# Row keys in the scatter's ring: from GpSimd's casts to a transfer of SyncE's

## The chip, the core and the metric

The kernel runs on one core of a Trainium2 chip. The metric is the device time of one execution in microseconds (us). The core's engines named here are TensorE (PE in the rows), VectorE (DVE), ScalarE (ACT), GpSimd (POOL) and SyncE (SP), which only issues DMA transfers. An indirect DMA is issued from GpSimd, and its descriptors are made there, so that each one is an instruction of that engine with a duration of its own; a plain DMA that SyncE issues is an instruction of SyncE's queue.

## What is computed

The model is a graph network with 6250 nodes of 256 features and 200,000 edges of 128 features. The part that the change touches is the first message sum: every edge's features are projected and added up at the edge's source node, and two tables are looked up by in-degree and out-degree.

```python
in_deg = jnp.minimum(jax.ops.segment_sum(ones, dst, num_segments=num_nodes), MAX_IN_DEGREE - 1)
out_deg = jnp.minimum(jax.ops.segment_sum(ones, src, num_segments=num_nodes), MAX_OUT_DEGREE - 1)
edge_proj = edge_attr @ W_sum + b_sum
sum3d = jax.ops.segment_sum(edge_proj, src, num_segments=num_nodes)
...
return x + z_in[in_deg] + z_out[out_deg] + cent_term + vor_term + sum3d
```

`src` is not sorted. Linear attention, a routed feed-forward layer, a second graph layer, a second attention and a mixture of experts follow; none of their code changes.

## The kernel before

**Section 1, sorting (to about 72 us).** The edge numbers lie as 128 partitions by 1568 columns (`EC`; 1562 columns are full, `EF`, and one more holds the tail of 64 edges). VectorE turns the source ids into fp32 keys (`src_f`, the first `EC` columns of the large tile `XT`) and into blocks of 125 nodes (`hi_src`), raises `hi_ready`, and counts how many edges fall into each block. It also copies the ids into the tile `pair`. SyncE loads the ids and `x`, writes a few padding rows to memory (line 357 and 358), and waits for all of that and for a barrier (line 304).

**Section 2, scatter, degree counts and attention.** The edges' rows are brought into the order of their source block by a scatter to the memory tensor `rows_by_src`. A row there has 129 words: 128 features and the source id as a key, by which a later stage builds one-hot tiles. What happens at once:

- SyncE loads features into a ring of three slots (`RINGS`), each of 11 columns (`HC`), that is 11 rows of 129 words in each partition. A slot's load waits until the eleven scatters that read it have landed (`ring_out`). There are 143 such units (`UNITS`); the last has one column.
- GpSimd's function `put_keys(n)` casts the 11 ids a partition of unit n from `pair` into word 128 of the slot's rows (line 609). It is called for unit n+1 behind the first scatter of unit n. Each unit then has 11 indirect DMAs (line 619), one a column, each of 128 rows of 516 bytes: 1563 in all.
- VectorE ranks the edges within their blocks in four chunks of columns (`CHUNKS`, lines 672 to 696), which gives the addresses `pos_src` of the scatter: a chunk must be ranked (`ranked`) before the first scatter of its columns. Then it makes one-hot tiles (`hots`) for the degree counts: 262 groups, each of two TENSOR_TENSOR instructions (lines 647 and 650), whose products TensorE sums (line 900). When all groups are done, it copies the counts (line 711), and the rest of the section (statistics, q, k and v, attention) follows from there as one chain.

The ranking and most of the one-hot work run beside the scatter. The section ends with a barrier, and the next one reads `rows_by_src`.

Of the kernel before, what the change touches and what calls it, by code (L numbers as in the profile page):

```python
# [12 lines left out]
F32 = mybir.dt.float32  # L13
# [9 lines left out]
N, D, E, ED = 6250, 256, 200000, 128  # L23
P = 125
NT = N // P
Q = 128
EF = E // Q
TAIL = E - Q * EF
EC = -(-(EF + 1) // 32) * 32
# [57 lines left out]
def bcast_rows(ap, rows):  # L87

    return ap.rearrange("(a d) -> a d", a=1).to_broadcast([rows, ap.shape[0]])


def program(nc, a, out):
# [3 lines left out]
    def sem(name):  # L96
        uid[0] += 1
        section.append(nc.alloc_semaphore(f"{name}_{uid[0]}"))
        return section[-1]
# [7 lines left out]
    def sbuf(ctx, name, shape, dt=F32):  # L107
        return ctx.enter_context(nc.sbuf_tensor(name, shape, dt))
# [19 lines left out]
                                                        skip_runtime_bounds_check_because="the tables are clamped where they are made")[1]  # L128


    counts_d = nc.dram_tensor("degree_counts", (2, ABREAST, HI * LOW), F32, kind="Internal").ap()
    rows_d = nc.dram_tensor("rows_by_src", (E + W1 + Q * EPAD, ED + 1), F32, kind="Internal").ap()
    pairs_d = nc.dram_tensor("pairs_by_dst", (E + W1 + Q * EPAD, 2), I32, kind="Internal").ap()
# [157 lines left out]
    src_f, dst_f = XT[:, 0 * EC:1 * EC], XT[:, 1 * EC:2 * EC]  # L291
# [3 lines left out]
    pair = sbuf(s01, "pair", [Q, EC * 2], I32)  # L295
# [8 lines left out]
    with ExitStack() as ctx:  # L304
# [14 lines left out]
        row = sbuf(ctx, "row", [1, NW2])  # L319
# [13 lines left out]
        ids_in, x_in, iotas, pads = (sem(s) for s in ("ids_in", "x_in", "iotas", "pads"))  # L333
        falls_ready, falls_summed = sem("falls_ready"), sem("falls_summed")
        counted, summed, pads_set = sem("counted"), sem("summed"), sem("pads_set")
        hi_ready, signs_summed = sem("hi_ready"), sem("signs_summed")
        src_tools = (mask, cnt, tot, first, col, col_i, cum, row, win_f, ps, counted, summed)
        block = ctx.enter_context(nc.Block())

        @block.sync  # L340
        def _(sp):
            for ids, name in ((src_i, "src"), (dst_i, "dst")):
                sp.dma_start(ids[:, 0:EF], a[name][0:Q * EF].rearrange("(p c) -> p c", c=EF)).then_inc(ids_in, 16)
            dst2 = a["dst"][0:Q * EF].rearrange("(p c) -> p c", c=EF)
            sp.wait_ge(pads_set, 3)
            with nc.allow_non_contiguous_dma(reason="one number a partition"):
                for ids, name in ((src_i, "src"), (dst_i, "dst")):
                    sp.dma_start(ids[0:TAIL, EF:EF + 1], a[name][Q * EF:E].rearrange("(p c) -> p c", c=1)).then_inc(ids_in, 16)
                sp.dma_start(next_i[0:Q - 1, 0:1], dst2[1:Q, 0:1]).then_inc(ids_in, 16)
                sp.dma_start(next_i[Q - 1:Q, 0:1], a["dst"][Q * EF:Q * EF + 1].rearrange("(p c) -> p c", c=1)).then_inc(ids_in, 16)  # L350
                sp.dma_start(next_i[0:TAIL - 1, 1:2], a["dst"][Q * EF + 1:E].rearrange("(p c) -> p c", c=1)).then_inc(ids_in, 16)
            for lo, hi in EVEN_ROWS:
                sp.dma_start(R[lo:hi, :].rearrange("p (t d) -> p t d", d=TS),
                             a["x"].rearrange("(t p) d -> p t d", p=P)[lo:hi]).then_inc(x_in, 16)

            sp.wait_ge(pads_set, 7)
            sp.dma_start(rows_d[E:E + W1, :].rearrange("(p r) c -> p (r c)", p=128), pad[:]).then_inc(pads, 16)
            sp.dma_start(pairs_d[E:E + W2, :].rearrange("(p r) c -> p (r c)", p=128), pad_i[:]).then_inc(pads, 16)
            sp.wait_ge(pads, 32)
            sp.wait_ge(x_in, 32)  # L360
            sp.wait_ge(pads_set, 8)

        @block.gpsimd
        def _(pool):
# [100 lines left out]
    with s01, ExitStack() as ctx:  # L465
        HC, RINGS = 11, 3
        UNITS = -(-(EF + 1) // HC)
# [46 lines left out]
        weights_in, mix_w_in, v_ones = sem("weights_in"), sem("mix_w_in"), sem("v_ones")  # L514
        ring_in = [sem(f"ring_in{h}") for h in range(RINGS)]
        ring_out = [sem(f"ring_out{h}") for h in range(RINGS)]
        keys_put = sem("keys_put")
        pos_dst, dst_mask = XT[:, 2 * EC:3 * EC].bitcast(I32), XT[:, 3 * EC:4 * EC].bitcast(BF16)
        dst_rank, dst_pos_f = XT[:, 0:EC], XT[:, EC:2 * EC]
        pair_stage = sbuf(ctx, "pair_stage", [Q, 2 * 8], I32)  # L520
# [3 lines left out]
        rank_step, ranked = sem("rank_step"), sem("ranked")  # L524
# [10 lines left out]
        block = ctx.enter_context(nc.Block())  # L535
        attr = a["edge_attr_128"][0:Q * EF, :].rearrange("(p c) d -> p c d", c=EF)
        ring4 = ring[:].rearrange("p (h c w) -> p h c w", h=RINGS, c=HC)
        pair_w = pair[:].rearrange("p (c w) -> p c w", w=2)

        @block.sync  # L540
        def _(sp):
            def load(n):
                h, count = n % RINGS, min(HC, EF - n * HC)
                if n >= RINGS:
                    sp.wait_ge(ring_out[h], n // RINGS * 16 * HC)
                if count:
                    sp.dma_start(ring4[:, h, 0:count, 0:ED], attr[:, n * HC:n * HC + count, :]).then_inc(ring_in[h], 16)
                if count < HC:
                    sp.dma_start(ring4[0:TAIL, h, count, 0:ED], a["edge_attr_128"][Q * EF:E, :]).then_inc(ring_in[h], 16)

            for n in range(RINGS):
                load(n)
            sp.dma_start(w_qkv[:].rearrange("p (k n) -> p k n", k=2), a["L0_mix_Wqkv"].rearrange("(k p) n -> p k n", p=128)).then_inc(mix_w_in, 16)
            sp.dma_start(w_out[:].rearrange("p (k n) -> p k n", k=2), a["L0_mix_Wout"].rearrange("(k p) n -> p k n", p=128)).then_inc(mix_w_in, 16)
            for j, name in enumerate(("W_cent", "b_cent", "W_vor", "b_vor")):
                v = a["L0_gnn_" + name]
                v = v.rearrange("a d -> (a d)") if len(v.shape) == 2 else v
                sp.dma_start(wcv[:, j * D:(j + 1) * D], bcast_rows(v, P)).then_inc(weights_in, 16)
            sp.dma_start(b_sum[:], bcast_rows(a["L0_gnn_b_sum"], P)).then_inc(weights_in, 16)
            sp.dma_start(gamma[:], bcast_rows(a["L0_mix_gamma"], P)).then_inc(weights_in, 16)  # L560
            with nc.allow_non_contiguous_dma(reason="one number a node"):
                for j, name in enumerate(("node_vec1_n2", "node_vec1")):
                    sp.dma_start(nvec[:, j * NT:(j + 1) * NT], a[name].rearrange("(t p) a -> p (t a)", p=P)).then_inc(weights_in, 16)
            falls = sp.value_load(unsorted[0:1, 0:1], min_val=0, max_val=E)
            with sp.If(falls == 0):
                sp.dma_start(pairs_d[0:Q * EF, :].rearrange("(p c) w -> p (c w)", p=Q), pair[:, 0:2 * EF]).then_inc(pairs_out, 16)
                sp.dma_start(pairs_d[Q * EF:E, :], pair[0:TAIL, 2 * EF:2 * EF + 2]).then_inc(pairs_out, 16)
                sp.wait_ge(pairs_out, 32)

            for n in range(RINGS, UNITS):  # L570
                load(n)

        @block.gpsimd
        def _(pool):
# [26 lines left out]
                for h in range(2):  # L601
                    pool.wait_ge(pair_out[h], 128 * (EC // 16))

            def put_keys(n):

                h, count = n % RINGS, min(HC, EF + 1 - n * HC)
                two_loads = n == UNITS - 1 and count > 1
                pool.wait_ge(ring_in[h], 16 * (n // RINGS + 1 + two_loads))
                pool.tensor_copy(ring4[:, h, 0:count, ED], pair_w[:, n * HC:n * HC + count, 0]).then_inc(keys_put, 1)

            pool.wait_ge(ranked, 1)
            put_keys(0)
            for n in range(UNITS):
                pool.wait_ge(keys_put, n + 1)
                for c in range(n * HC, min((n + 1) * HC, EF + 1)):
                    for k in range(1, len(CHUNKS)):
                        if c == CHUNKS[k][0]:
                            pool.wait_ge(ranked, k + 1)
                    pool.indirect_dma_start(rows_d, bass.IndirectOffsetOnAxis(ap=pos_src[:, c:c + 1].bitcast(U32), axis=0),  # L619
                                            ring4[:, n % RINGS, c - n * HC, :], None).then_inc(ring_out[n % RINGS], 16)  # L620
                    if c == n * HC and n + 1 < UNITS:
                        put_keys(n + 1)
            for h in range(RINGS):
                pool.wait_ge(ring_out[h], 16 * sum(min(HC, EF + 1 - n * HC) for n in range(h, UNITS, RINGS)))
            falls = pool.value_load(unsorted[0:1, 0:1], min_val=0, max_val=E)
# [4 lines left out]
        def _(dve):  # L630
# [141 lines left out]
            def q_share(t):  # L772

                s3, _, qs = q_parts(t)
                dve.wait_ge(qexp_ready, t + 1)
                ch.step(dve.tensor_reduce(qs, s3, AX.X, ALU.add))
                ch.step(dve.reciprocal(qs, qs))
                dve.tensor_tensor(s3, s3, qs.unsqueeze(2).to_broadcast([P, HEADS, HD]), ALU.mult).then_inc(qn_ready, 1)
# [419 lines left out]
    with ExitStack() as ctx:  # L1198
# [17 lines left out]
        key = prod[:, 0:3 * NT]  # L1216
# [1253 lines left out]
```

## Time and profile before

| what | value |
|---|---|
| time, median of 3 runs | 7276.67 us (7267.32 to 7280.35) |
| time of the profiled execution | 7325.64 us |
| its span, first to last instruction | 7323.8 us |
| mean granted TensorE clock | 0.886 |
| busy: PE, DVE, POOL, ACT | 3721.2, 3396.8, 3665.4, 697.5 us |
| the scatter (line 619), first to last start | 125.2 to 2310.6 us |
| the last one-hot group (line 647) starts | 2604.4 us |

No engine is busy for more than half of the span or so, because different stages have different limits; so the reader has to look at one stage, from 125 to 2607 us, and ask there who is waited for. The profiled execution is 49 us longer than the median of the timed runs; a difference worked out from the profile is taken from both.

### The profile page before, as it was taken

Reading aid. Unit: us, or ns where it says so; the run is one execution under the profiler, and the core shown is the slowest. Engines: PE = TensorE matmul, PEld = TensorE weight load, DVE = VectorE, ACT = ScalarE, POOL = GpSimd, SP = SyncE. Lnnn points to the kernel's source line nnn. Section 1 sums busy time; section 2 is a strip of 40 time slices with the busy share of each in tenths; the row PEclk is TensorE's granted clock in tenths of the full one; section 3 lists DMA queues with packets and bytes.
Section 4 is the critical chain, followed back from the end, with each engine's and each line's share of the span. In section 5 each row is a group of like instructions: output and inputs, shape, how many; then the busy total and the mean of one; then the engine's idle time right before and its main releaser. Section 6 shows DMA issues by size and latency. Waiting matters only on the chain. (4 is left out here: it accounts for less than half of the span.)

```text
span 7323.8 us, 57084 instructions
## 1 busy us (share of the span) xinstructions
PE 3721.2 (51%) x15758; PEld 2691.5 (37%) x15758; DVE 3396.8 (46%) x6601; ACT 697.5 (10%) x1555; POOL 3665.4 (50%) x3859
## 2 busy tenths in 40 slices
PE   0000111111113639699899655565655556655796
PEld 0000000000001215489788433333334444434685
DVE  8335422222225995688833445454433333337413
ACT  7000000000000022200132100000000000003232
POOL 2767766776664000086000466666666666650353
PEclk9999999999999999899999877777777767656898
DMA  4333333333331000089500433333333333352124
GB/s 105 99 90 95 95 94 93 93 95 94 95 94 50 0 2 1 1 316 320 165 1 3 108 87 86 90 89 87 91 87 93 91 90 91 90 75 89 44 72 151
DMA packets 577434, 661.05 MB, mean 90 GB/s; under 512 B 214086, under 2 KB 447368, under 8 KB 576930
## 3 DMA queue, kind: packets, MB, share of 16 engines
q0 software_dynamic: 145440, 364.03, 17.3%
q1 hardware_dynamic: 365790, 286.62, 13.5%
q10 hardware_dynamic: 65956, 7.55, 0.7%
q8 instruction: 100, 1.64, 0.1%
q14 instruction: 148, 1.21, 0.1%
HBM read 518.48 MB, written 139.39 MB: 90 GB/s over the span
## 5 line engine op out<-in xcount | busy, mean ns | idle before, releaser
L1629 POOL DMA_INDIRECT rows<-projected_rows,pw_in x1664 | 1612.3, 969 | 931.1 <-issue 477.1
L619 POOL DMA_INDIRECT rows_by_src<-ring,pos_src x1563 | 1506.9, 964 | 642.3 <-issue 637.0
L1876 PE MATMUL pg<-rows,hot 128*125 128x256 f32 x3328 | 1121.7, 486 | 969.8 <-DVE hot L1719 535.7
L1876 PEld LDWEIGHTS pg<-rows,hot 128*125 128x125 f32 x3328 | 736.2, 237 | 1348.3 <-DVE hot L1719 656.1
L900 PE MATMUL pqkv<-hots 128*126 128x450 bf16 x1042 | 458.6, 595 | 1311.3 <-issue 845.0
L1644 DVE TENSOR_TENSOR agg<-agg,pg 125x256 f32 x832 | 347.2, 417 | 1442.1 <-remote 862.8
L900 PEld LDWEIGHTS pqkv<-hots 128*126 128x126 bf16 x1042 | 193.3, 216 | 1577.3 <-issue 918.8
L647 DVE TENSOR_TENSOR hots<-pctx,src_low 128x1800 bf16<-128x1800 f32 x131 | 264.9, 2022 | 971.4 <-remote 810.4
L1138 PE MATMUL pw<-hot,win 128*128 128x125 f32 x3968 | 454.9, 277 | 80.0 <-DVE hot L1082 78.9
L1138 PEld LDWEIGHTS pw<-hot,win 128*128 128x128 f32 x3968 | 449.1, 193 | 86.0 <-DVE hot L1082 79.3
L1037 POOL MEMSET acc<- 128x6375 f32 x1 | 5.4, 5411 | 812.0 <-POOLq L104 812.0
L1719 DVE SCALAR_TENSOR_TENSOR hot<-pw_in,m_block_first,g_numbers 128x250 f32<-128x250 int32 x832 | 391.0, 470 | 31.8 <-DMA m_bl<-in_L_gnn_b_l 14.4
L255 PE MATMUL pqkv<-d_cnt,lower 128*128 128x50 f32 x2 | 0.7, 434 | 746.4 <-issue 746.4
L1082 DVE SCALAR_TENSOR_TENSOR hot<-win,win_base,iota_f 128x1000 f32<-128x1000 f32 x248 | 335.0, 1351 | 17.6 <-issue 9.3
L647 DVE TENSOR_TENSOR hots<-pctx,XT 128x1800 bf16<-128x1800 f32 x131 | 263.3, 2010 | 118.6 <-remote 85.7
L255 PEld LDWEIGHTS pqkv<-d_cnt,lower 128*128 128x128 f32 x2 | 0.5, 312 | 746.8 <-issue 746.8
L676 DVE TENSOR_TENSOR_SCAN pqkv<-XT,first_src,pctx 128x448 f32<-128x448 bf16 (+2 forms) x200 | 207.3, 1037 | 141.7 <-remote 64.1
L189 ACT ACT_TABLE_LOAD x3 | 3.8, 1283 | 2459.1 <-DMA degree_counts<-hots 2459.1
L681 DVE COPY_PREDICATED XT<-XT,pqkv 128x448 f32<-128x448 uint16 (+2 forms) x200 | 118.2, 591 | 215.2 <-remote 138.8
L2383 PE MATMUL e_ph<-XT 128*128 128x256 f32 x896 | 204.4, 382 | 1.5 <-ACT XT L2345 0.8
L2394 PE MATMUL e_py<-e_w,XT 128*128 x896 | 202.5, 379 | 0.0
L2291 POOL DMA_INDIRECT XT<-moe_rows,e_row_from x112 | 109.5, 978 | 185.5 <-SPq L2263 151.7
(430 smaller groups left out, 5711.4 us busy)
## 6 DMA issues: line engine op xcount, KB each, us to landing
win<-rows_by_src SPq DMA_DIRECT2D x248, 516.0 KB
ring<-in_edge_attr SPq DMA_DIRECT2D x142, 704.0 KB
rows<-projected_rows,pw_in POOLq DMA_INDIRECT x1664
rows_by_src<-ring,pos_src POOLq DMA_INDIRECT x1563
XT<-moe_results SPq DMA_DIRECT2D x25, 448.0 KB
e_w<-in_L_ffn_W SPq DMA_DIRECT2D x16, 512.0 KB
pw_in<-pairs_by_dst SPq DMA_DIRECT2D x432, 2.0 KB
pw_in<-pairs_by_dst ACTq DMA_DIRECT2D x400, 2.0 KB
```

The source lines that it names most:

```text
L619: pool.indirect_dma_start(rows_d, bass.IndirectOffsetOnAxis(ap=pos_src[:, c:c + 1].bitcast(U32), axis=0), ring4[:, n % RINGS, c - n * HC, ...
L647: dve.tensor_tensor(hots[:, o:o + width * LOW].rearrange("p (c n) -> p c n", c=width), numbers[:, 0:LOW].unsqueeze(1).to_broadcast([Q, wid ...
L676: step("scan", b, dve.tensor_tensor_scan(pqkv[:, b % 4, 0:n], masks[:, b % 4, 0:n], pctx[:, 0, 0:n], first_src[:, b:b + 1], ALU.add, ALU.b ...
L900: mm = pe.matmul(pqkv[0:ABREAST * HI, which, 0:ABREAST * LOW], hots[:, o + LO + j * HI:o + LO + (j + ABREAST) * HI], hots[:, o + j * LOW:o ...
L1082: dve.scalar_tensor_tensor(out=hot[:, (s % 4) * R1 * P:(s % 4 + 1) * R1 * P].rearrange("p (r n) -> p r n", r=R1), in0=keys.unsqueeze(2).to ...
L1138: mm = pe.matmul(pw[:, s % 4, 0:P], win[:, s * RC + r * (ED + 1):s * RC + r * (ED + 1) + ED], hot[:, ((s % 4) * R1 + r) * P:((s % 4) * R1 ...
L1629: pool.indirect_dma_start(rows[:, (2 * (s % RU) + r) * D:(2 * (s % RU) + r + 1) * D], None, proj_d, bass.IndirectOffsetOnAxis(ap=pairs_of( ...
L1644: dve.tensor_tensor(tile, tile, pg[0:P, bank, 0:D], ALU.add).then_inc(acc_done, 1)
L1719: dve.scalar_tensor_tensor(out=hot[:, (s % 4) * 2 * P:(s % 4 + 1) * 2 * P].rearrange("p (r n) -> p r n", r=2), in0=keys.unsqueeze(2).to_br ...
L1876: mm = pe.matmul(pg[0:P, s % 4, 0:D], hot[:, ((s % 4) * 2 + r) * P:((s % 4) * 2 + r + 1) * P], rows[:, (2 * (s % RU) + r) * D:(2 * (s % RU ...
L2383: mm = pe.matmul(ph[:, m, 0:MW], w1s[:, (2 * (t % 2) + k) * EXP_H + m * 128:(2 * (t % 2) + k) * EXP_H + (m + 1) * 128], xT[:, (2 * (t % 2) ...
L2394: mm = pe.matmul(py[:, v, 0:D], hT[:, (t % 2 * NH + m) * MW + v * 128:(t % 2 * NH + m) * MW + (v + 1) * 128], w2[:, bass.ds((e * NH + m) * ...
```

## The change

A new memory tensor `source_keys` receives the fp32 keys `src_f` in section 1, by one transfer of 128 rows of 1568 words. In section 2, each load of a ring slot is followed by a second transfer on the same queue and to the same semaphore, which takes the unit's keys from `source_keys` (11 consecutive words in each of 128 partitions) and puts each into word 128 of its row. `put_keys`, its 143 casts and its semaphore are gone. GpSimd now waits, at the start of a unit, until both transfers of the slot have landed.

```diff
+    keys_d = nc.dram_tensor("source_keys", (Q, EC), F32, kind="Internal").ap()
...
+            sp.wait_ge(hi_ready, 1)
+            sp.dma_start(keys_d[:, :], src_f).then_inc(keys_out, 16)
             sp.wait_ge(pads_set, 7)
...
             sp.wait_ge(pads_set, 8)
+            sp.wait_ge(keys_out, 16)
...
                 if count:
                     sp.dma_start(ring4[:, h, 0:count, 0:ED], attr[:, n * HC:n * HC + count, :]).then_inc(ring_in[h], 16)
+                keys = min(HC, EF + 1 - n * HC)
+                with nc.allow_non_contiguous_dma(reason="one key a row"):
+                    sp.dma_start(ring4[:, h, 0:keys, ED], keys_d[:, n * HC:n * HC + keys]).then_inc(ring_in[h], 16)
                 if count < HC:
...
-            def put_keys(n):
-
-                h, count = n % RINGS, min(HC, EF + 1 - n * HC)
-                two_loads = n == UNITS - 1 and count > 1
-                pool.wait_ge(ring_in[h], 16 * (n // RINGS + 1 + two_loads))
-                pool.tensor_copy(ring4[:, h, 0:count, ED], pair_w[:, n * HC:n * HC + count, 0]).then_inc(keys_put, 1)
-
             pool.wait_ge(ranked, 1)
-            put_keys(0)
             for n in range(UNITS):
-                pool.wait_ge(keys_put, n + 1)
-                for c in range(n * HC, min((n + 1) * HC, EF + 1)):
+                h, count = n % RINGS, min(HC, EF + 1 - n * HC)
+                three_loads = n == UNITS - 1 and count > 1
+                pool.wait_ge(ring_in[h], 32 * (n // RINGS + 1) + 16 * three_loads)
+                for c in range(n * HC, n * HC + count):
...
                     pool.indirect_dma_start(rows_d, bass.IndirectOffsetOnAxis(ap=pos_src[:, c:c + 1].bitcast(U32), axis=0),
-                                            ring4[:, n % RINGS, c - n * HC, :], None).then_inc(ring_out[n % RINGS], 16)
-                    if c == n * HC and n + 1 < UNITS:
-                        put_keys(n + 1)
+                                            ring4[:, h, c - n * HC, :], None).then_inc(ring_out[h], 16)
```

In GpSimd's order, at the start of the scatter, these are the rows of before (CAST writes the keys into the ring, DMA is one indirect DMA of the scatter, its shape that of the whole target):

```order
L575 MEMSET v_one 125x774
L576 MEMSET neg_kmax 128x256
L609 CAST ring<-pair 128x11
L619 DMA rows_by_src<-ring,pos_src 201792x129
L609 CAST ring<-pair 128x11
L619 DMA rows_by_src<-ring,pos_src 201792x129 x11
L609 CAST ring<-pair 128x11
```

and these are the rows of the change, with what each waits for:

```order
L581 MEMSET neg_kmax 128x256
L618 DMA rows_by_src<-ring,pos_src 201792x129 [waits ring_in0_31,ranked_44]
L618 DMA rows_by_src<-ring,pos_src 201792x129 x10
L618 DMA rows_by_src<-ring,pos_src 201792x129 [waits ring_in1_32]
L618 DMA rows_by_src<-ring,pos_src 201792x129 x10
```

No cast stands between scatters any more, and the wait for the ring stands at the first scatter of the unit itself, where before it stood at the cast, one unit earlier.

In SyncE's order, behind the section's small loads, these are the rows of before:

```order
L567 DMA pairs_by_dst<-pair 64x2
L565 UNCONDITIONAL_BRANCH [waits pairs_out_39]
L547 DMA ring<-in_edge_attr 128x11x128 [waits ring_out0_33]
L547 DMA ring<-in_edge_attr 128x11x128 [waits ring_out1_34]
L547 DMA ring<-in_edge_attr 128x11x128 [waits ring_out2_35]
```

and these the rows of the change:

```order
L572 DMA pairs_by_dst<-pair 64x2
L570 UNCONDITIONAL_BRANCH [waits pairs_out_39]
L549 DMA ring<-in_edge_attr 128x11x128 [waits ring_out0_34]
L552 DMA ring<-source_keys 128x11x1
L549 DMA ring<-in_edge_attr 128x11x128 [waits ring_out1_35]
```

Each load of the ring now has a transfer of 1408 single words behind it, which has no wait of its own.

## Rows read from the trace of the kernel before

**Rows 1.** The page: the largest groups of GpSimd.
```profile
L1629 POOL DMA_INDIRECT rows<-projected_rows,pw_in x1664 | 1612.3, 969 | 931.1 <-issue 477.1
L619 POOL DMA_INDIRECT rows_by_src<-ring,pos_src x1563 | 1506.9, 964 | 642.3 <-issue 637.0
```

**Rows 2.** Groups by line, VectorE, window 842 to 2313 us.
```profile
L647 DVE TENSOR_TENSOR hots<-pctx,src_low 128x1800 bf16<-128x1800 f32 x131 | 264.9, 2022 | 971.4 <-remote 810.4 <-issue 160.9
L650 DVE TENSOR_TENSOR hots<-pctx,src_high 128x504 bf16<-128x504 f32 x131 | 87.7, 669 | 0.0
```

**Rows 3.** Waits, VectorE, window 842 to 2313 us: total, times, longest.
```profile
DVE hots L647 <- remote: 888.0, 115, 9.3
```

**Rows 4.** Windows of line 647: before and after the last scatter (second number: busy us).
```profile
842.80:2313.20 1470.40, 295.31 (x146) 1.00 0.32 93
2313.20:2605.30 292.10, 232.84 (x116) 1.00 0.00 0
```

**Rows 5.** Timeline, VectorE, end of the degree count.
```profile
2606.72 1.16 DVE L711 COPY hots<-pqkv 126x450 f32<-126x450 f32 x2 [1.50 <-PE pqkv L900]
```

**Rows 6.** Line 619 alone: shortest/median/longest ns, first and last start.
```profile
L619 POOL DMA_INDIRECT rows_by_src<-ring,pos_src x1563: 953/962/1690, 125.2 to 2310.6; - x196
```

**Rows 7.** Line 609 alone, the same.
```profile
L609 POOL CAST ring<-pair x143: 201/213/244, 124.7 to 2294.8; 128x11 f32<-128x11 int32 x142, 128x1 f32<-128x1 int32 x1
```

**Rows 8.** Timeline, GpSimd: the first two casts between scatters.
```profile
125.20 1.15 POOL L619 DMA_INDIRECT rows_by_src<-ring,pos_src  x1 [0.29 <-POOL ring L609]
126.36 0.21 POOL L609 CAST ring<-pair 128x11 f32<-128x11 int32 x1
126.73 0.99 POOL L619 DMA_INDIRECT rows_by_src<-ring,pos_src  x1 [0.16 <-issue]
...
139.52 0.97 POOL L619 DMA_INDIRECT rows_by_src<-ring,pos_src  x1 [0.30 <-issue]
140.48 0.22 POOL L609 CAST ring<-pair 128x11 f32<-128x11 int32 x1
140.86 0.99 POOL L619 DMA_INDIRECT rows_by_src<-ring,pos_src  x1 [0.16 <-issue]
```

**Rows 9.** Timeline, GpSimd: a cast beside slow scatters.
```profile
1322.01 0.96 POOL L619 DMA_INDIRECT rows_by_src<-ring,pos_src  x1 [0.30 <-issue]
1322.97 0.22 POOL L609 CAST ring<-pair 128x11 f32<-128x11 int32 x1
1324.39 0.98 POOL L619 DMA_INDIRECT rows_by_src<-ring,pos_src  x1 [1.20 <-issue]
1326.48 0.96 POOL L619 DMA_INDIRECT rows_by_src<-ring,pos_src  x1 [1.11 <-issue]
```

**Rows 10.** Timeline, GpSimd: the last cast.
```profile
2293.84 0.96 POOL L619 DMA_INDIRECT rows_by_src<-ring,pos_src  x1 [0.30 <-issue]
2294.80 0.20 POOL L609 CAST ring<-pair 128x1 f32<-128x1 int32 x1
2296.63 0.98 POOL L619 DMA_INDIRECT rows_by_src<-ring,pos_src  x1 [1.62 <-issue]
```

**Rows 11.** Timeline, SyncE, the last instruction that it issues for the ring.
```profile
2280.91 0.50 SPq L549 DMA_DIRECT2D ring<-in_edge_attr  x1
```

**Rows 12.** Timeline, SyncE, early in the program.
```profile
24.94 3.46 SPq L357 DMA_DIRECT2D rows_by_src<-pad  x1
```

**Rows 13.** Waits of SyncE: waited for, total us, times, longest.
```profile
SPq L304 <- PEq L304: 28.7, 1, 28.7
```

**Rows 14.** Timeline, SyncE, start of the section with the scatter.
```profile
86.21 11.77 SPq L563 DMA_DIRECT2D nvec<-in_node_vec  x1
...
140.53 0.39 SPq L547 DMA_DIRECT2D ring<-in_edge_attr  x1
```

**Rows 15.** DMA queues, window 90 to 98 us.
```profile
q1 hardware_dynamic: 6153, 0.11, 45.8%
```

**Rows 16.** DMA queues, window 1307 to 1315 us.
```profile
q1 hardware_dynamic: 1424, 0.72, 33.6%
```

More of the change, by code:

```diff
@@ L335, in program @@
         counted, summed, pads_set = sem("counted"), sem("summed"), sem("pads_set")
-        hi_ready, signs_summed = sem("hi_ready"), sem("signs_summed")
+        hi_ready, signs_summed, keys_out = sem("hi_ready"), sem("signs_summed"), sem("keys_out")
         src_tools = (mask, cnt, tot, first, col, col_i, cum, row, win_f, ps, counted, summed)
@@ L516, in program @@
         ring_out = [sem(f"ring_out{h}") for h in range(RINGS)]
-        keys_put = sem("keys_put")
         pos_dst, dst_mask = XT[:, 2 * EC:3 * EC].bitcast(I32), XT[:, 3 * EC:4 * EC].bitcast(BF16)
@@ L537, in program @@
         ring4 = ring[:].rearrange("p (h c w) -> p h c w", h=RINGS, c=HC)
-        pair_w = pair[:].rearrange("p (c w) -> p c w", w=2)
         @block.sync
@@ L602, in scatter_pairs_all @@
                     pool.wait_ge(pair_out[h], 128 * (EC // 16))
-            def put_keys(n):
+            pool.wait_ge(ranked, 1)
+            for n in range(UNITS):
                 h, count = n % RINGS, min(HC, EF + 1 - n * HC)
-                two_loads = n == UNITS - 1 and count > 1
-                pool.wait_ge(ring_in[h], 16 * (n // RINGS + 1 + two_loads))
-                pool.tensor_copy(ring4[:, h, 0:count, ED], pair_w[:, n * HC:n * HC + count, 0]).then_inc(keys_put, 1)
-            pool.wait_ge(ranked, 1)
-            put_keys(0)
-            for n in range(UNITS):
-                pool.wait_ge(keys_put, n + 1)
-                for c in range(n * HC, min((n + 1) * HC, EF + 1)):
+                three_loads = n == UNITS - 1 and count > 1
+                pool.wait_ge(ring_in[h], 32 * (n // RINGS + 1) + 16 * three_loads)
+                for c in range(n * HC, n * HC + count):
                     for k in range(1, len(CHUNKS)):
```

## The prediction

> **What bounds the kernel now.** I read the page first, then the stage of the scatter by its groups of instructions, then windows, and last the timeline one instruction at a time.
>
> The page's groups put the scatter's 1563 indirect DMAs among the two largest pieces of GpSimd's work: 1506.9 us busy and 642.3 us idle ahead of them, of which 637.0 us is "issue", that is, nothing that the profile shows was waited for [rows 1]. They run without a break from 125.2 to 2310.6 us [rows 6]. That is 1562 intervals from start to start in 2185.4 us, 1.399 us each, where the busy part is 0.96.
>
> The one-hot groups of VectorE run beside them, and the reader should see two paces in the windows. Until the last scatter 146 groups take 1470.4 us, 10.07 us a group; behind it 116 groups take 292.1 us, 2.52 us a group [rows 4]. The first of a group's two instructions takes 2.02 us, and in the slow stretch VectorE sat idle ahead of it for 971.4 us in the first 131 groups, mostly "remote" [rows 2]; the longest of these waits is 9.3 us [rows 3]. TensorE is done with a group before VectorE makes the next, so VectorE is waiting for GpSimd to let it in, and it stops waiting when the scatter stops. The last group starts at 2604.4 us, the count is copied at 2606.72 us [rows 5], and the rest of the section hangs on that.
>
> So the end of the stage is the end of the scatter, P, and behind it the groups that are then left: end = P + (262 - g) x 2.52, with g the groups done by P. If P comes earlier by 1 us, 1/10.07 of a group is left over for the fast stretch, which gives back 0.25 us. **A microsecond saved on the scatter is worth 0.75 us at the end.** What follows waits for this chain, so I carry it on one to one.
>
> **What is removed.** GpSimd's 143 casts take 213 ns each by the median [rows 7], 30 us in all. That is not their price, since a scatter of 0.97 us leaves an idle gap of 0.30 us behind it anyway [rows 8], 1.27 us from start to start. The price is read from the interval between the two scatters around a cast. At the start of the stage it is 1.53 and 1.34 us (125.20 to 126.73, 139.52 to 140.86) [rows 8]. At 1322 us it is 2.38 us, and the next interval is 2.09 us [rows 9]. At the very last cast it is 2.79 us [rows 10]. I laid all starts of the timeline in a row: the 142 intervals that hold a cast, the first and the last being those just named, have a mean of 2.00 us; the 142 that follow them have a mean of 1.49; the other 1278 have 1.32. (142 x 2.00 + 142 x 1.49 + 1278 x 1.323 = 2186, the measured 2185.4.)
>
> Is it the cast or the load that SyncE issues at nearly the same time? SyncE's last instruction for the ring is at 2280.91 us [rows 11], 14 us ahead of the last cast, which still had its 2.79 us [rows 10]. And the second cast cost nearly nothing although loads were being issued then too: one at 140.53 us [rows 14], within that interval. So I hold the cast dear, and not the load. What it pays for I take to be a second contest with VectorE for the way into the memory: it is cheap where VectorE happens not to be asking.
>
> The Trainium skill (SBUF — State Buffer, Who interferes with whom) has GpSimd and VectorE share one pair of ports as an exclusive lock, whoever starts first blocking the other for the whole instruction, and lets a VectorE instruction with at most one SBUF input, outside the two-port modes, never contend. Line 647 reads one operand from PSUM and one from SBUF, so by that sentence it would not wait; the trace says that it does, by 971.4 us over 131 groups [rows 2]. By the rule the 262 groups would take 2.52 us each from 842.8 us and be done at 1503 us, P alone would set the end, and the gain would be the whole of P's. I go by the trace.
>
> **The sum.** Without casts I take the pace of the 1278 intervals that neither hold nor follow one: 1562 x 1.323 = 2066 us, 119 us less than 2185.4. Times 0.75 this is 89 us. The bounds of this pace, from both sides:
>
> - dearest: an interval with a cast costs only what the second cast shows above 1.27, 0.07 us, and what lies around the others belongs to VectorE's requests and stays. 142 x 0.07 = 10 us, times 0.75 = 7 us.
> - cheapest: every interval goes to 1.27 us. (1.399 - 1.27) x 1562 = 201 us, times 0.75 = 151 us. The gathers of line 1629, which have no cast between them, come near it: they idle for "issue" for 477.1 us over 1664, 0.29 us each, against 637.0 us over 1563, 0.41 us, here [rows 1].
>
> I stay with 1.32, in between, because it is measured in this very stage, with VectorE's same requests around it. It may still hold some after-effect of casts, so I would sooner expect more than less.
>
> **What is added.** (1) In section 1 a write of 784 KB behind the loads of `x`, ahead of the padding writes that SyncE issues at 24.94 us [rows 12]. SyncE then sat for 28.7 us at the barrier, waiting for VectorE's counts [rows 13]. The write is somewhat larger than one load of the ring, which I price at 3 us below, so it costs nothing; without that cover it would be some 4 us. VectorE raises the semaphore that it waits for long before 24.94 us.
>
> (2) 143 transfers of 1408 words. The nearest thing in the trace are the two loads of one word a node: in 8 us 6153 packets went through [rows 15], 1.3 ns a packet, so 1408 take about 2 us. A ring load's 1424 packets kept the engines busy for a third of 8 us, about 3 us [rows 16]. Both must land before the slot is used, and a unit takes 11 x 1.32 = 14.5 us. The load is issued when the slot is free, which is one scatter into the next unit; before, the cast wanted it one unit later, now the scatter wants it two units later, some 28 us. So 2 us more has 23 us of cover. SyncE's queue is in order: behind the new transfer stands the next load, which waits for its own slot 14 us later. The new issues cost SyncE 0.4 us each, or up to a few us for one (11.77 for the 6250 words of the second of those loads [rows 14]); the small loads behind the first three are then some us late. They were issued by 98 us (86.21 + 11.77), and only the copy of the pairs stands between them and the fourth load of the ring at 140.53 us [rows 14], so these few us lie in a gap.
>
> (3) GpSimd's wait at a unit's start is for transfers that landed long before, so it adds nothing. The first scatter waits for the first rank, at 125 us, not for the ring.
>
> **The rivals.**
> - *The casts are not the cause, or their room is taken by something else* (chance 0.12). VectorE's requests would then stretch every scatter by the same amount, the pace stays at 1.40 throughout, and 0 to 7 us is won: 7270 to 7277. For it: pieces of the timeline do run at 1.40 without a cast near. Against it: the interval with the cast is the longest of the unit, also where no load is issued.
> - *More comes back* (0.08): the after-effects of a cast spread over the unit, the pace goes to between 1.27 and 1.29, and 128 to 151 us is won (7126 to 7149). For it: the pace of the gathers.
> - *VectorE is let in less often* (0.06), the case on the other side. GpSimd's long pauses at the casts are also VectorE's openings. Let P be 2194 and VectorE need d us a group from 843 us on. The end is 2194 + (262 - 1351 / d) x 2.52. At 10.07 it is 2516; at 13.7 it is 2605, no gain; at 16 it is 2641, or 7313 for the whole. So it decides from 13.7 us a group. Against it: the longest of its 115 "remote" waits is 9.3 us [rows 3], which makes 12 us a group, and the openings that I saw it take lie at all places of a unit.
>
> **How the numbers follow.** The likeliest case has 0.74. Its own range is a pace of 1.30 to 1.36, 61 to 155 us of scatter, 46 to 116 us at the end: 7161 to 7231. The time is 7276.7 - 89 = 7188 us (in a profiled execution 7325.6 - 89 = 7237). The range that should hold it 8 times in 10 takes in the near part of the neighbouring cases: 7145 to 7250. A measurement of this kernel can tell about 0.2%, 15 us, from no change. Faster by more: 0.74 + 0.08 = 0.82. Within: 0.12. Slower by more: 0.06.
>
> **What would show it.** In the profile after: no cast in GpSimd's groups; the last scatter starts near 2192 us and the mean interval is 1.32; the interval at the second scatter of a unit is no longer than the others; the one-hot groups keep about 10 us before the last scatter and 2.5 behind it; some 135 are done by then; the count is copied near 2518 us. The prediction is wrong if the interval behind a unit's first scatter stays near 2 us (then it was the load, and there are now two), if the other intervals rise to 1.40, or if the groups slow down to 13 us.

## The result, and the profile after

The changed kernel takes 7323.2 us (median of 5, 7317.7 to 7329.5) where the kernel before, run beside it, takes 7280.4 us: a ratio of 1.006, with a 95% interval of 1.0047 to 1.0073. It is 43 us slower; 89 us faster had been forecast. Every ratio in this document compares fast executions with fast ones, and one of the four executions of "neither" below, at 8994 us, is left out of its ratio for that.

The profiled execution of the changed kernel has a span of 7316.2 us, less than the 7323.8 of before. The profiled execution of before was taken apart from the timed ones and lies 45 us above their median. Behind the copy of the degree counts it is 45 us longer than that of the changed kernel, and the gathers of the second graph layer, whose code is the same in both, take 49 us more in it (2473.7 against 2424.3 us from first to last start). So the two are compared stage by stage, up to the copy of the degree counts. The experiments below repeat that comparison with both sides on one chip.

The views of single lines of the changed kernel (its scatter is line 618, its large one-hot instruction 644, the cast of the ranks to `pos_src` 693, the copy of the counts 708; columns as in [rows 6]):

```profile
L618 POOL DMA_INDIRECT rows_by_src<-ring,pos_src x1563: 964/972/1887, 125.2 to 2285.5; - x196
...
L693 DVE CAST pos_src<-XT x4: 259/394/409, 124.7 to 835.2; 128x448 int32<-128x448 f32 x2, 128x192 int32<-128x192 f32 x1, 128x480 int32<-128x480 f32 x1
...
L708 DVE COPY hots<-pqkv x2: 617/622/628, 2644.0 to 2644.6; 126x450 f32<-126x450 f32 x2
```

The last two of these lines for before, which ahead of the prediction were not shown as groups:

```profile
L696 DVE CAST pos_src<-XT x4: 259/393/409, 124.3 to 804.7; 128x448 int32<-128x448 f32 x2, 128x192 int32<-128x192 f32 x1, 128x480 int32<-128x480 f32 x1
...
L711 DVE COPY hots<-pqkv x2: 614/620/626, 2606.7 to 2607.3; 126x450 f32<-126x450 f32 x2
```

The last scatter starts 25 us earlier than in [rows 6], not 119. The last chunk is ranked 30 us later (835.2 against 804.7). The counts are copied 37 us later (2644.0 against 2606.7). These 37 us are nearly all of the 43 us by which the time grew, and the rest is less than one profile can tell.

The windows of line 644 (second number: busy us, then how many instructions touch the window) answer to [rows 4], and the wait to [rows 3]:

```profile
878.70:2286.00 1407.30, 260.58 (x129) 1.00 0.37 93
2286.00:2313.00 27.00, 4.39 (x4) 1.00 0.01 3
2313.00:2645.00 332.00, 263.05 (x131) 1.00 0.00 0
```

```profile
DVE hots L644 <- remote: 907.1, 106, 9.3
```

VectorE begins its groups at 878.7 us (before: 842.8), and needs 11.0 us a group until the last scatter (before: 10.07). Behind 2313 us it needs 2.5 again. The stretch between is new: the scatter is over at 2286.5 us, but VectorE is still held up for some 27 us. The timeline of VectorE shows it:

```profile
2285.64 2.03 DVE L644 TENSOR_TENSOR hots<-pctx,src_low 128x1800 bf16<-128x1800 f32 x1 [8.58 <-remote]
...
2296.14 2.03 DVE L644 TENSOR_TENSOR hots<-pctx,src_low 128x1800 bf16<-128x1800 f32 x1 [7.88 <-remote]
...
2306.64 0.63 DVE L644 TENSOR_TENSOR hots<-pctx,src_low 128x450 bf16<-128x450 f32 x1 [7.88 <-remote]
...
2312.94 2.03 DVE L644 TENSOR_TENSOR hots<-pctx,XT 128x1800 bf16<-128x1800 f32 x1 [5.48 <-remote]
```

In the kernel before, the last long wait ends at nearly the same moment, although its scatter ran 25 us longer:

```profile
2313.22 2.03 DVE L647 TENSOR_TENSOR hots<-pctx,XT 128x1800 bf16<-128x1800 f32 x1 [7.88 <-remote]
```

So the time from which VectorE runs free did not move with the scatter. What moved is how many groups were left at it: 262 - 146 = 116 before [rows 4], 131 now. Fifteen groups more at 2.52 us are 38 us, and the counts are copied 37 us later.

The timeline of GpSimd shows that the slow intervals of the scatter did not go away with the casts. They stand elsewhere in the unit, here at its fourth scatter, and a part of them is now inside the instruction (1.21 and 1.10 us in place of 0.97):

```profile
1302.47 1.03 POOL L618 DMA_INDIRECT rows_by_src<-ring,pos_src  x1 [0.30 <-issue]
1304.39 1.21 POOL L618 DMA_INDIRECT rows_by_src<-ring,pos_src  x1 [0.89 <-issue]
1305.90 1.10 POOL L618 DMA_INDIRECT rows_by_src<-ring,pos_src  x1 [0.30 <-issue]
1307.31 0.98 POOL L618 DMA_INDIRECT rows_by_src<-ring,pos_src  x1 [0.30 <-issue]
```

### The profile page after: what moved, and what is told of

It reads as the page before. It is cut to its first block and busy times, and to the rows that moved or that the text cites. A ratio compares the mean times of both kernels' runs of the same rounds, so it can differ in the third digit from the quotient of the medians.

```text
span 7316.2 us, 57086 instructions
## 1 busy us (share of the span) xinstructions
PE 3749.5 (51%) x15758; PEld 2701.9 (37%) x15758; DVE 3399.8 (46%) x6601; ACT 697.6 (10%) x1555; POOL 3747.3 (51%) x3716
## 3 DMA queue, kind: packets, MB, share of 16 engines
q14 instruction: 148, 1.21, 0.1%
## 5 line engine op out<-in xcount | busy, mean ns | idle before, releaser
L618 POOL DMA_INDIRECT rows_by_src<-ring,pos_src x1563 | 1633.7, 1045 | 579.1 <-issue 527.6
```

## The experiments

Two theories stood at the start. A: the casts let VectorE in, and without them it is held out longer. B: the new transfers (1408 single words a unit, and twice the issues of SyncE) slow the stage. The runs were spread over several chips, and every ratio is against the kernel before on the same chip. On the chips of the first eight experiments the kernel before took 7313 us (both, neither, the casts on ScalarE, two casts) and 7319 us (the other four).

**Both.** The changed kernel, with a cast a unit back on GpSimd whose result nothing reads:

```diff
                                             ring4[:, h, c - n * HC, :], None).then_inc(ring_out[h], 16)
+                    if c == n * HC and n + 1 < UNITS:
+                        if n:
+                            pool.wait_ge(keys_cast, n)
+                        pool.tensor_copy(spare_keys[:], pair[:].rearrange("p (c w) -> p c w", w=2)[:, n * HC:(n + 1) * HC, 0]).then_inc(keys_cast, 1)
```

> The changed kernel, with its transfers of keys, and with one cast a unit put back on GpSimd behind the unit's first scatter; the cast writes into a spare tile that nothing reads. Theory A (the casts were VectorE's openings): VectorE goes back to about 10.1 us a one-hot group and is done ranking near 805 us, the count is copied at 2600 to 2615 us, and the time is that of before within 0.2%. Theory B (the new transfers slow the stage): VectorE stays near 11 us a group, the scatter grows, the count is copied at 2640 us or later, and the time is 1.006 of before or more.

Measured: 1.0006 of before (0.9996 to 1.0016). The ranks are done at 805.5 us, and the counts are copied where they were before:

```profile
L699 DVE CAST pos_src<-XT x4: 260/394/410, 124.5 to 805.5; 128x448 int32<-128x448 f32 x2, 128x192 int32<-128x192 f32 x1, 128x480 int32<-128x480 f32 x1
...
L714 DVE COPY hots<-pqkv x2: 617/622/627, 2605.9 to 2606.5; 126x450 f32<-126x450 f32 x2
```

With all the transfers in place, a useless cast takes the loss back. That is theory A. For B the interval leaves at most 0.16%, 12 us.

**Neither.** The kernel before without casts and without transfers; the keys are set to zero once, so the first message sum comes out wrong. GpSimd's wait for the load of the ring stays, once a unit:

```diff
             pool.memset(neg_kmax[:], 0.0).then_inc(v_ones, 1)
+            pool.memset(ring4[:, :, :, ED], 0.0).then_inc(keys_put, 1)
...
-                pool.tensor_copy(ring4[:, h, 0:count, ED], pair_w[:, n * HC:n * HC + count, 0]).then_inc(keys_put, 1)
```

> The kernel before without the casts and without any transfer of keys: the keys in the ring are set to zero once, so the output lacks the first message sum. Theory A: as the changed kernel, 11 us a group, the count copied near 2644 us, 1.005 to 1.007 of before. Theory B: 10 us a group and a scatter at 1.32 us an interval, the count copied at 2520 to 2560 us, 0.985 to 0.993 of before.

Measured: 1.0061 (1.0041 to 1.0082), as theory A had it. The scatter and the copy stand at the times of the changed kernel, and on one chip with "both" they are 39 us apart (2605.9 and 2644.8):

```profile
L619 POOL DMA_INDIRECT rows_by_src<-ring,pos_src x1563: 964/974/2532, 125.1 to 2285.9; - x196
...
L709 DVE COPY hots<-pqkv x2: 614/620/626, 2644.8 to 2645.4; 126x450 f32<-126x450 f32 x2
```

**The casts on ScalarE.** The kernel before, with `put_keys` moved to ScalarE (three units ahead of its other work, the rest behind it):

```diff
-                pool.tensor_copy(ring4[:, h, 0:count, ED], pair_w[:, n * HC:n * HC + count, 0]).then_inc(keys_put, 1)
...
+                act.copy(ring4[:, h, 0:count, ED], pair_w[:, n * HC:n * HC + count, 0]).then_inc(keys_put, 1)
```

> The kernel before with the casts of the keys on ScalarE, which is idle in this stretch, in place of GpSimd; no transfer of keys. Theory A: as the changed kernel, 11 us a group, 1.005 to 1.007 of before. Theory B: 0.985 to 0.993 of before.

Measured: 1.008 (1.0064 to 1.0097), the counts copied at 2644.9 us. A third way to keep the casts off GpSimd, with the same end of the stage. The ratio is above the 1.007 that had been expected at most. The rest lies in the gathers of the second graph layer: 2485.9 us from first to last start, where "neither" has 2471.6; why they took longer is open.

**Two casts a unit.** The kernel before with one useless cast more, behind the seventh scatter:

```diff
                     if c == n * HC and n + 1 < UNITS:
                         put_keys(n + 1)
+                    if c == n * HC + 6:
+                        if n:
+                            pool.wait_ge(keys_cast, n)
+                        pool.tensor_copy(spare_keys[:], pair_w[:, n * HC:(n + 1) * HC, 0]).then_inc(keys_cast, 1)
```

> The kernel before with a second cast a unit, into a spare tile, behind the unit's seventh scatter. If a cast costs the 0.67 us by which its interval is longer, the scatter is some 95 us longer. Theory A: VectorE gains by it, to about 9.3 us a group, and the net is near 40 us, 1.005 of before. Theory B: VectorE keeps 10.07 us a group, and the net is 73 us, 1.010 of before.

Measured: 0.9943 (0.9924 to 0.9961), faster than before, where both theories had expected it slower (1.005 or 1.010). VectorE's pace was as theory A had it, 9.34 us a group. But the second cast did not cost the scatter the 95 us of the expectation: its last start is at 2311.3 us, as with one.

```profile
L621 POOL DMA_INDIRECT rows_by_src<-ring,pos_src x1563: 952/958/2533, 125.5 to 2311.3; - x196
...
L702 DVE CAST pos_src<-XT x4: 259/394/409, 124.6 to 753.6; 128x448 int32<-128x448 f32 x2, 128x192 int32<-128x192 f32 x1, 128x480 int32<-128x480 f32 x1
...
L717 DVE COPY hots<-pqkv x2: 615/620/626, 2562.2 to 2562.8; 126x450 f32<-126x450 f32 x2
```

**More of them.** The same with casts at other places: for e5 `if c > n * HC`, ten more a unit; for e6 three more, `if (c - n * HC) in (3, 6, 9)`; e8 is e5 with `spare_keys[:, 0:1]` and one column of `pair`.

> The kernel before with a cast behind every scatter but the last of a unit's own place: the unit's own cast and ten into a spare tile. By the counts so far (none: 11.0 us a group; one: 10.1; two: 9.3, with no longer scatter) theory A, that each cast is an opening for VectorE, has VectorE at 6 us a group or less, done ranking before 600 us, and the count copied before 2400 us, 0.97 of before. Rival C, that each further cast costs GpSimd as it does where VectorE asks for the way (0.5 to 1.5 us), has the scatter 700 us or more longer, and the time above that of before.

> The kernel before with four casts a unit, three of them into a spare tile behind the fourth, seventh and tenth scatter. Theory A: 8.3 us a group or less, the count copied at 2480 to 2530 us, 0.983 to 0.990 of before. Rival C: the second cast was free by chance, the third and fourth make the scatter 95 us longer each, and the time is that of the kernel before or above.

> As e5_every, but each of the ten additional casts has one column in place of eleven. If the opening lies in the instruction and not in its width, the paces are those of e5_every and the time is the same within 0.3%, since a cast of one column took 0.20 us and one of eleven 0.21. If it lies in the time that GpSimd spends, they still agree. If only wide ones open, this is the slower one.

Measured: e5 0.9321 (0.930 to 0.9343), e6 0.979 (0.9771 to 0.9809), e8 0.9327 (0.9304 to 0.9351). e5 and e6 are below what theory A had expected (0.97, and 0.983 to 0.990), e8 agrees with e5 as expected. The effect can be read off as a dose. For 0, 1, 2, 4 and 11 casts a unit the ranks are done at 835, 805, 754, 673 and 501 us, and the counts are copied at 2644, 2607, 2562, 2461 and 1920 us, while the last scatter starts at 2286, 2311, 2311, 2319 and 2343 us. Rival C had 700 us more of scatter for e5; it is 32. The 687 us by which e5 copies the counts earlier are not all won: the rest of its section now runs beside the scatter and waits there too (between 1920 and 2640 us VectorE has 105.3 us and ScalarE 109.7 us of "remote" in one line each), and the next section begins 497 us earlier (its first one-hot at 2631 us in place of 3128). Of e5:

```profile
L621 POOL DMA_INDIRECT rows_by_src<-ring,pos_src x1563: 974/980/1929, 125.5 to 2343.1; - x196
...
L703 DVE CAST pos_src<-XT x4: 259/394/409, 124.7 to 501.0; 128x448 int32<-128x448 f32 x2, 128x192 int32<-128x192 f32 x1, 128x480 int32<-128x480 f32 x1
...
L718 DVE COPY hots<-pqkv x2: 616/621/626, 1920.1 to 1920.6; 126x450 f32<-126x450 f32 x2
```

The width of the cast does not matter within the intervals (e8). Even with eleven, VectorE waits before line 654, the one-hot instruction, for 345 us in 131 groups, by the groups of VectorE from 500 to 1925 us; with one it was 971.4 us [rows 2]:

```profile
L654 DVE TENSOR_TENSOR hots<-pctx,src_low 128x1800 bf16<-128x1800 f32 x131 | 264.6, 2020 | 344.9 <-remote 198.2 <-PE pqkv L907 119.8 <-issue 26.8
```

What a cast does is not to let VectorE in at that moment. In the trace of before, 3 of the 146 groups that start before the last scatter do so within 1.5 us behind a cast; starts spread evenly over the unit would give some 14. What nearly holds through all these traces is a count. Between the starts of two groups, while the scatter runs, GpSimd starts this many instructions by the mean, as counted from the timelines:

| casts a unit | us from group to group | indirect DMAs a group | all GpSimd instructions a group |
|---|---|---|---|
| 0 (the changed kernel; neither) | 10.99; 10.99 | 7.86; 7.85 | 7.86; 7.85 |
| 1 (before; both) | 10.07; 10.11 | 7.18; 7.23 | 7.83; 7.89 |
| 2 | 9.36 | 6.69 | 7.90 |
| 4 | 7.87 | 5.60 | 7.64 |
| 11 | 5.30 | 3.75 | 7.50 |

So a cast counts nearly as an indirect DMA does, and costs far less time than one. Why there are some 8 to a group, these runs don't show.

**Not a cast.** The changed kernel with a MEMSET at the place of e1's cast:

```diff
+                    if c == n * HC:
+                        if casts[0]:
+                            pool.wait_ge(keys_cast, casts[0])
+                        pool.memset(spare_keys[:], 0.0).then_inc(keys_cast, 1)
+                        casts[0] += 1
```

> The changed kernel with one instruction of GpSimd a unit behind the first scatter, but a MEMSET of the spare tile, which reads nothing, where e1_both had the cast. If any instruction of GpSimd's own between two scatters opens the way, this is the time of before, as e1_both: 10.1 us a group, the count copied near 2607 us. If the reading of memory is what matters, it stays at 11 us and 2644 us.

Measured: 1.0011 (0.9999 to 1.0023), the ranks done at 805.4 us and the counts copied at 2603.7 us, as in e1, with 7.86 instructions of GpSimd a group. Reading memory is not what matters; an instruction of the engine between two indirect DMAs is enough. A wait that is met at once is not: the changed kernel and "neither" have one a unit, for the ring.

**On the changed kernel, on the gathers, and a pause without an instruction.** e9 is the changed kernel with a MEMSET of one column behind every scatter, e10 the same behind every gather too, e11 the changed kernel with one load of a register a unit:

```diff
+                    if c == n * HC and n + 1 < UNITS:
+                        pool.value_load(unsorted[0:1, 0:1], min_val=0, max_val=E)
```

> The changed kernel, with its transfers of keys, and a MEMSET of one column into a spare tile behind every scatter. Theory A (an instruction of GpSimd's own between two scatters lets VectorE in, and the transfers cost nothing): the time of e5_every within 0.5%, 0.93 of before. Theory B in a weaker form (the transfers do cost, but it is hidden while VectorE is the one that is late): the scatter is 50 us or more longer than the 2343 us of e5_every, though this shows in the time only if the section ends on it.

> e9_changed_every with the same MEMSET behind every one of the 1664 gathers of the second graph layer. Theory A, if it holds for gathers as for scatters: VectorE's wait ahead of its additions there, 1387.7 us in the changed kernel, falls by some hundred us, and that stage ends at least 50 us earlier; 0.92 of before or less. Against it: that stage may be bound by GpSimd's own 1664 x 1.27 us, and each MEMSET adds 0.07 us, 116 us in all; then the time is that of e9_changed_every or up to 116 us more.

> The changed kernel with one load of a register by GpSimd's sequencer a unit behind the first scatter (0.51 us in the trace of before, at the end of the scatter), in place of the cast of e1_both: a pause, but no instruction of the engine proper. If the time between two scatters is the opening, VectorE goes back to 10.1 us a group and the count is copied near 2607 us. If it takes an instruction of the engine, it stays at 11 us, and the count is copied at 2644 us or later.

None of the expectations that tell the theories apart could be put to the test: measured are 0.9989, 0.9999 and 0.9978, but of another number, since on this chip the kernel before takes 6001 us. They were run again with the changed kernel itself beside them:

> The changed kernel itself, beside the three of the last call, whose chip ran the kernel before in 6001 us. On a chip where VectorE is held out of the scatter (before near 7300 us): 1.005 to 1.007 of before, 11 us a group. On one where it is not (before near 6000 us): 2.5 us a group, a scatter near 2137 us, and 0.2% less than before, which is 143 casts at 0.07 to 0.1 us.

> e11_register_load again, since its first run was on a chip where VectorE was not held out. Where before takes 7300 us: if a pause opens the way, 10.1 us a group and 1.000 of before; if it takes an instruction of the engine, 11 us a group and 1.006.

> e9_changed_every again. Where before takes 7300 us: 0.93 of before, as e5_every, if the transfers of keys cost nothing; a scatter 50 us or more longer than 2343 us if they do. Where before takes 6000 us: 0.999 as in its first run.

> e10_gathers_too again. Where before takes 7300 us: 0.92 or less if VectorE is held out beside the gathers as beside the scatter; the time of f3_changed_every or up to 116 us more if that stage is bound by GpSimd's own instructions.

Measured: 0.998 (0.9971 to 0.999), 0.9979, 0.9987 and 0.9999, of 6003 us, on one more chip of the same sort. And once more, with the kernel before traced:

> e11_register_load once more. Where before takes 7300 us: if a pause opens the way, 10.1 us a group and 1.000 of before; if it takes an instruction of the engine, 11 us a group and 1.006. Where before takes 6000 us: 0.998, as twice before.

> e9_changed_every once more. Where before takes 7300 us: 0.93 of before, as e5_every, if the transfers of keys cost nothing. Where before takes 6000 us: 0.999, as twice before.

> The kernel before itself, for its trace. Where before takes 7300 us: 10.1 us a group and a mean interval of 1.40 us, as in the trace that the prediction used. Where it takes 6000 us: 2.5 us a group from the first to the last, a count copied near 1100 us, and intervals with a cast that are only 0.07 us longer than the others, since nobody contends.

Measured, on a third chip of that sort: 0.9974 (0.9964 to 0.9985), 0.9985 (0.9975 to 0.9994) and 1.0001, of 6003 us. The views of single lines of the kernel before, from its trace there:

```profile
L619 POOL DMA_INDIRECT rows_by_src<-ring,pos_src x1563: 954/958/2922, 125.6 to 2139.4; - x196
...
L696 DVE CAST pos_src<-XT x4: 260/412/499, 124.7 to 414.5; 128x448 int32<-128x448 f32 x2, 128x192 int32<-128x192 f32 x1, 128x480 int32<-128x480 f32 x1
...
L711 DVE COPY hots<-pqkv x2: 617/622/627, 1099.1 to 1099.6; 126x450 f32<-126x450 f32 x2
```

The same program, and the counts are copied at 1099 us in place of 2607. VectorE has no wait ahead of line 647 at all, 2.5 us a group from the first, and its ranking and GpSimd's scatter run side by side:

```profile
L647 DVE TENSOR_TENSOR hots<-pctx,src_low 128x1800 bf16<-128x1800 f32 x131 | 263.5, 2011 | 0.0
```

The interval around the cast below, from the timeline, is 1.34 us; by the mean over all, intervals with a cast take 1.36 us and the others 1.28:

```profile
139.87 0.97 POOL L619 DMA_INDIRECT rows_by_src<-ring,pos_src  x1 [0.30 <-issue]
140.84 0.21 POOL L609 CAST ring<-pair 128x11 f32<-128x11 int32 x1
141.21 0.98 POOL L619 DMA_INDIRECT rows_by_src<-ring,pos_src  x1 [0.15 <-issue]
```

So VectorE is held out in the runs with 7300 us and not in those with 6000 us. Each chip was used once, and all runs with 7300 us came before all with 6000 us, so these runs don't tell a difference between chips from something else that changed in between; "sort of chip" stands for both here. The changed kernel is 0.6% slower on the one sort and 0.2% faster on the other. e9, e10 and e11 say nothing of the first sort, where they never ran: whether a pause alone would let VectorE in, whether the transfers cost anything once it is let in everywhere, and what the gathers would gain, is open. Against the pause there is one number from e5: uncontended, a cast and the idle time behind it take 0.37 us where an idle gap of 0.30 us stood anyway, and yet the groups of VectorE come twice as often as without casts.

## Why the prediction was wrong

**The reading of what bounds the stage held in part.** The stage ends on VectorE's groups, a group takes 2.52 us once VectorE is free, and what follows moved with it.

**The step that failed is "Without casts I take the pace of the 1278 intervals that neither hold nor follow one".** I took the excess at the casts for their price. The scatter's mean interval went from 1.399 to (2285.5 - 125.2) / 1562 = 1.383 us, not to 1.32; "neither" has the same without any transfer. So most of the excess is not the casts'. It goes with VectorE's work beside the scatter, since where VectorE never waits the mean interval is 1.289 us, with casts and without; and it is paid somewhere in the unit whatever stands between the scatters. By place in the unit, the intervals of before have a mean of 2.00 and 1.49 us behind the first two scatters and 1.28 to 1.38 behind the others; those of "neither" have 1.35 to 1.42 everywhere. That a second cast cost nothing (2311.3 us) and ten more 32 us says the same: a cast's own price is small, as it is at the start of the stage [rows 8] and on the chips where nobody contends. The argument from the last cast, that it was the cast and not the load [rows 10, 11], told apart two wrong candidates and left the third out.

**The second step that failed, the one that turned the sign, is the pace of 10.07 us a group, held fixed.** The rival "VectorE is let in less often" was the right one, and had 0.06. That without the casts VectorE gets in less often is shown by e1, e2 and the dose. Its reason, that GpSimd's pauses at the casts are the openings, is not: groups do not start at the casts, and what stays the same is the number of GpSimd's instructions a group. I ruled it out by its price: at the P that I forecast, it decided only from 13.7 us a group, and the longest wait gave 12. With the P that came, 11.0 was enough. I had also priced the groups alone: VectorE's ranking in front of them is held out in the same way, and came 30 us later.

**The third step that failed is "A microsecond saved on the scatter is worth 0.75 us at the end".** It took the last scatter for the moment at which VectorE comes free. In before, changed, both, neither, the casts on ScalarE, two casts and MEMSET, the last scatter starts at 2286 us (without an instruction between them) or at 2309 to 2311 us (with one or two), and the last long wait of VectorE ends at 2312 to 2315 us in all seven. An earlier end of the scatter was worth nothing here; only the number of groups done by 2313 us counted.

In the terms of the sum: P 25 us earlier, times 0.75, is -19 us. The first group 36 us later (36 / 10.07 x 2.52) is +9. The pace of 10.99 over some 1407 us is 11.7 groups fewer, +29. The stretch behind the last scatter, 27 us with 3 groups where some 11 would fit, is +17 net of the 3 us that before has there too. Together +36, where +37 was measured; the sum had no term for this stretch.

**What is added cost nothing that could be measured, as forecast**: e1, which has all of the transfers and the casts, is the time of before within 0.16%. GpSimd's wait at the start of a unit shows no idle time: all that stands ahead of line 618 is "issue" (527.6 us over 1562, the longest 0.9), but for the wait for the first rank.

**The range** was built from prices of the cast alone. The lower bound of the gain, 7 us, had been read from an interval with no contention, and it was the nearest of the bounds to what the casts cost the scatter (10 us there, 25 us measured); it got little weight because the mean over 142 intervals looked like the better measurement. A mean is no price where another engine's requests are in it. But all bounds were gains, and the range had no room for a loss.

The rule of the Trainium skill (SBUF — State Buffer, Who interferes with whom), by which line 647 would not contend, is contradicted by every trace with 7300 us (971.4 us of waits in 131 groups of the kernel before, "remote" for the most part) and agrees with that of the kernel before with 6000 us, where line 647 never waits.

## What to carry to other kernels

An instruction beside which another engine waits can be worth more than it costs: before removing it, ask what the other engine does in that moment, and price the removal by the pace of that engine, not by the gap around the instruction. Where VectorE waits for "remote" beside a long row of indirect DMAs, put one small instruction of GpSimd's own behind every one of them and look: a cast behind each scatter was 6.8% faster here than the kernel before, a cast of one column did as well as one of eleven, and with one a unit a MEMSET did as well as a cast. Where VectorE is not held out, a MEMSET behind each scatter of the changed kernel cost some 7 us (5996.7 against 5989.7 us on one chip), and was still no slower than the kernel before (0.9985 to 0.9989). And repeat a result of a few tenths of a per cent on a second chip and at another time, since this one has the other sign there.

## What was not expected of the hardware

- The same kernel, the one before, takes 7267 to 7332 us in the first three sets of runs (two chips, and that of the result, which may be a third) and 5995 to 6010 us in three later ones on three other chips. In the traces the whole difference lies in two stretches with indirect DMAs: up to the first gather, 971 us (4082.0 or 3110.9 us; the degree counts are copied at 2607 or at 1099 us), and in the gathers, 350 us (2474 or 2124 us from first to last start). Together they are the 1321 us between the spans.
- On the first sort VectorE remained held out for some 27 us behind the last indirect DMA when no other instruction of GpSimd's engine had stood among them (changed kernel, "neither", the casts on ScalarE), and 2 to 7 us when one or two a unit had. The waits there are as long as beside the scatter, 7.88 us, while GpSimd issues nothing, and the DMA engines move 0.07 MB in those 27 us. So what holds VectorE out is neither the indirect DMA's own duration nor its traffic. What it is, these runs don't show.
- In the kernel before, VectorE's groups start at distances that cluster at 9.8, 10.5, 11.2 and 11.9 us, 0.7 us apart, and the scatter's intervals at 1.27, 1.4, 2.1 and 2.8. Only the grid was seen, not its cause.
- On the second sort, on two chips, the changed kernel's scatter is no shorter (2013.4 us against 2013.8), since its indirect DMAs take 967 ns by the median where they took 958. Its 0.2% lie, by the two traces, in the gathers, whose code did not change: 2112.8 us from first to last start against 2123.9, 946 ns by the median against 953. That the duration of an indirect DMA differs by some ns from one program to another was seen in all traces; why, was not tried.
